# Swapping two PSUM banks in a pipelined attention stage: value transposes and value projection trade places

## The reference

```python
h = tok(x)                              # importance MLP, cumsum, pooling 750 -> 375 tokens a batch
h = h + attn(layernorm(h))              # 8 heads of 64
h = h + ffn(layernorm(h))               # 16 experts, top-k by expert, and a shared MLP
# attn, on xn = layernorm(..) * gamma + beta, padded with two zero columns in front:
y = wd0 * (W @ xn)[:-2] + wd1 * (W @ xn)[1:-1] + wd2 * (W @ xn)[2:]    # for q, k and v alike
p = softmax(q k^T * scale - slope * |i - j|, causal);  out = (p v) @ wout.T
# ffn: probs = softmax(layernorm(h) @ gate_w); each expert takes its best tokens
```

## Time and profile before

| what | value |
|---|---|
| median of 3 runs | 1337.28 us (1337.11 to 1339.53) |
| the profiled execution, its own time | 1337.11 us |
| its span, first to last instruction | 1335.4 us |
| PE busy over the span | 1181.6 us, 88% |
| PEld | 992.4 us, 74% |
| DVE | 895.8 us, 67% |
| ACT | 732.2 us, 55% |
| POOL | 405.9 us, 30% |
| mean granted TensorE clock | 0.956 of full speed |

### The profile page before, as it was taken

One profiled execution on the slowest core, in us unless ns is written; L12 is line 12 of the kernel. 1 busy time (PEld: TensorE's weight loads), 2 busy tenths in 40 slices (PEclk: granted clock), 3 DMA queues, 4 the chain that ended last, 5 costly groups with the idle time before them and its releaser, 6 DMA issues. The chain is left out here.

```text
span 1335.4 us, 23186 instructions
## 1 busy us (share of the span) xinstructions
PE 1181.6 (88%) x7812; PEld 992.4 (74%) x7812; DVE 895.8 (67%) x2614; ACT 732.2 (55%) x1845; POOL 405.9 (30%) x379
## 2 busy tenths in 40 slices
PE   6999999999978999999999999999995998766663
PEld 6999999999966777777777777777773777545552
DVE  5656566656658988888888888897874887222220
ACT  2444534344448877788877778887882432222220
POOL 5000001302011444333344323231111001688885
PEclk9999999999989999999999999999997998988876
DMA  5100000000010000000000000000002100444542
GB/s 140 31 13 24 12 24 12 18 19 12 1 36 1 19 18 17 26 26 26 25 19 11 23 27 26 25 11 11 14 16 55 30 18 19 100 91 89 90 87 23
DMA packets 91800, 42.94 MB, mean 32 GB/s; under 512 B 31066, under 2 KB 88007, under 8 KB 91687
## 3 DMA queue, kind: packets, MB, share of 16 engines
q1 hardware_dynamic: 67207, 33.49, 9.3%
q0 software_dynamic: 23808, 6.69, 3.9%
q10 hardware_dynamic: 672, 1.31, 0.3%
HBM read 28.22 MB, written 9.65 MB: 28 GB/s over the span
## 5 line engine op out<-in xcount | busy, mean ns | idle before, releaser
L487 PE MATMUL bank<-h1hl,W2hl 128*128 128x376 f32 x1536 | 277.3, 336 | 2.9 <-DVE h1hl L643 2.9
L487 PEld LDWEIGHTS bank<-h1hl,W2hl 128*128 128x128 f32 x1536 | 263.6, 189 | 7.4 <-issue 4.3
L1057 ACT ACTIVATE P<-P,nmax 125x375 f32<-125x375 f32 (+2 forms) x384 | 189.0, 501 | 1.4 <-DVE nmax L1185 1.4
L587 ACT ACTIVATE h<-bank,b2c 128x375 f32<-128x375 f32 x128 | 73.5, 575 | 207.3 <-PE bank L487 207.3
L226 POOL TENSOR_SCALAR cellmax<-grid,csb 125x375 f32<-125x375 f32 x96 | 122.7, 1288 | 206.0 <-DVE csb L219 133.1
L1185 DVE CUSTOM_DVE_ANT_0 P<-bank,nbias 125x375 f32<-125x375 f32 (+2 forms) x384 | 138.9, 410 | 2.1 <-PE bank L898 1.7
L1067 ACT COPY PT<-bank 128x500 f32<-128x500 f32 (+1 forms) x256 | 127.9, 553 | 6.5 <-PE bank L911 6.1
L898 PE MATMUL bank<-QK 64*125 64x375 f32 (+2 forms) x768 | 116.3, 407 | 4.2 <-DVE nmax L1185 3.7
L911 PE MATMUL bank<-ident,P 125*128 125x125 f32 x768 | 113.4, 275 | 0.6 <-ACT P L1057 0.4
L1075 ACT ACTIVATE tap<-bank,qkd 128x375 f32<-128x375 f32 x128 | 68.6, 571 | 79.2 <-PE bank L951 79.1
L1651 ACT ACTIVATE hE<-bank,EB 128x375 f32<-128x375 f32 x64 | 36.7, 573 | 134.8 <-PE bank L1600 132.0
(11 more groups left out here) (209 smaller groups left out, 2326.7 us busy)
## 6 DMA issues: line engine op xcount, KB each, us to landing
X<-in_x_dram SPq DMA_DIRECT2D x31, 375.0 KB
EW<-in_L_ffn_w_dram SPq DMA_DIRECT2D x32, 256.0 KB
token_table<-row SPq DMA_DIRECT2D x16, 210.9 KB
tTall<-tT SPq DMA_DIRECT2D x16, 187.5 KB, 2.5
out_dram<-oS SPq DMA_DIRECT2D x16, 187.5 KB
tTall<-in_L_tok_W_dram ACTq DMA_DIRECT2D x1, 1024.0 KB, 8.9
EB<-in_L_ffn_b_dram SPq DMA_DIRECT2D x16, 62.5 KB
tok<-token_table,ids POOLq DMA_INDIRECT x48
```

What stands on the lines that cost most here:

```text
L487: last = nc.tensor.matmul(bank[4 + m % 2][:, :NE], W2hl[:, a, k, m * 128:(m + 1) * 128], h1hl[:, p, b, k], start=(k == 0 and n == 0), stop ...
L587: nc.scalar.activation(h2[:, p, m], bank[4 + m % 2][:, :N], ACT.Gelu, bias=b2c[:, m:m + 1]).then_inc(s_g2, 1)
L1057: nc.scalar.activation(P[:, 2 * r + q, SEG[i]:SEG[i] + w], P[:, 2 * r + q, SEG[i]:SEG[i] + w], ACT.Exp, bias=nmax[:, 2 * r + q, i:i + 1], ...
```

## The change

The values trade banks, and two pieces of work move within their engines' lists:
- `transpose_v` writes G0 instead of G1 and ACT L1090 reads it there. It waits for the queries to be finished (`s_qk` 2c + 3) and no longer for the keys (2c + 4).
- `project_v` writes G1 instead of G0, waits until the keys' taps have been read out of it, and stands in PE's list behind `transpose_probs`. ACT's first tap of the values stands behind `copy_probs` accordingly, and DVE's taps read G1.
- `project_qk` swaps its waits: the queries now wait for the copied values and, for certain pairs, for the gate's reads of pTs and of the logits, and the keys wait for VT.
- The gate's transposed probabilities and logits go to G0 as well.
- `take_n2T` moves on ACT from the end of step 7 to the end of step 0 of the next body, and `split_n2T` on DVE from step 0 to step 1, ahead of `take_pooled`.

In the diff below the other edits only rename the bank: ACT's copy of the values (L1090), PE L1011 and L1039 and DVE L1268, L1283 and L1286 go from G1 to G0, and DVE's value taps (L1208, L1214) from G0 to G1.

```diff
@@ project_qk, project_v, transpose_v (PE) @@
                         if n == 0:
-                            wait(pe, s_vt, 4 * m + c)
-                        else:
                             wait(pe, s_v, 4 * m + c - 1)
                             if c == 2:
                                 wait(pe, s_pc, m - 1)
                             if c == 1:
                                 wait(pe, s_lm, 2 * (m - 1))
+                        else:
+                            wait(pe, s_vt, 4 * m + c)
...
                 def project_v(m, c, u):
-                    pe.wait_ge(s_qk, 8 * m + 2 * c + 1)
+                    pe.wait_ge(s_qk, 8 * m + 2 * c + 2)
...
-                        last = nc.tensor.matmul(G0[:, :XE], WVT[:, a, c * 128:(c + 1) * 128], xnThl[:, u, x_],
+                        last = nc.tensor.matmul(G1[:, :XE], WVT[:, a, c * 128:(c + 1) * 128], xnThl[:, u, x_],
...
                     pe.wait_ge(s_vt, 4 * m + c + 1)
-                    pe.wait_ge(s_qk, min(8 * m + 2 * c + 4, 8 * B))
+                    pe.wait_ge(s_qk, min(8 * m + 2 * c + 3, 8 * B))
...
-                        last = nc.tensor.transpose(G1[:PT_, t * 128:(t + 1) * 128], VT[:, t * PT_:(t + 1) * PT_],
+                        last = nc.tensor.transpose(G0[:PT_, t * 128:(t + 1) * 128], VT[:, t * PT_:(t + 1) * PT_],
@@ body (PE) @@
-                        if part == 1:
-                            if valid(b):
-                                transpose_v(b, c)
-                            if valid(m):
-                                project_v(m, d, m % 2)
-                        m, d = pair_before(b, c, 2)
-                        if part == 0 and valid(m):
-                            attend(m, d, u if c >= 2 else v_)
-                        m, d = pair_before(b, c, 1)
-                        if valid(m):
-                            transpose_probs(m, d, part)
+                        if part == 1 and valid(b):
+                            transpose_v(b, c)
+                        k, e = pair_before(b, c, 2)
+                        if part == 0 and valid(k):
+                            attend(k, e, u if c >= 2 else v_)
+                        k, e = pair_before(b, c, 1)
+                        if valid(k):
+                            transpose_probs(k, e, part)
+                        if part == 1 and valid(m):
+                            project_v(m, d, m % 2)
@@ body (ACT) @@
-                            if valid(m):
-                                act.wait_ge(s_vp, 4 * m + d + 1)
-                                wait(act, s_vt1, 4 * m + d)
-                                nc.scalar.activation(tap0[:, 2], G0[:, 0:N], ACT.Copy,
-                                                     scale=vd[:, d, 0:1]).then_inc(s_vt0, 1)
                         m, d = pair_before(b, c, 1)
                         if part == 1 and valid(m):
                             copy_probs(m, d, 1)
+                        k, e = next_pair(b, h)
+                        if part == 1 and valid(k):
+                            act.wait_ge(s_vp, 4 * k + e + 1)
+                            wait(act, s_vt1, 4 * k + e)
+                            nc.scalar.activation(tap0[:, 2], G1[:, 0:N], ACT.Copy,
+                                                 scale=vd[:, e, 0:1]).then_inc(s_vt0, 1)
...
-                        if h == 7 and ahead(b + 2):
-                            take_n2T(act, b + 2, G2)
+                        if h == 0 and ahead(b + 1):
+                            take_n2T(act, b + 1, G2)
@@ body (DVE) @@
-                        if h == 0 and ahead(b + 1):
+                        if h == 1 and ahead(b + 1):
                             split_n2T(dve, b + 1)

```

More of the change, by code:

```diff
@@ L1010, in body @@
                             for t in range(NT):
-                                last = nc.tensor.transpose(G1[:E, t * PT_:(t + 1) * PT_], row[:, t, C:ROW],
+                                last = nc.tensor.transpose(G0[:E, t * PT_:(t + 1) * PT_], row[:, t, C:ROW],
                                                            ident[:PT_, :PT_])
@@ L1038, in body @@
                             for t in range(NT):
-                                last = nc.tensor.matmul(G1[:PT_, t * E:(t + 1) * E], tT[:, t * PT_:(t + 1) * PT_],
+                                last = nc.tensor.matmul(G0[:PT_, t * E:(t + 1) * E], tT[:, t * PT_:(t + 1) * PT_],
                                                         gate[:], start=True, stop=True)
@@ L1090, in body @@
                                 nc.scalar.copy(V[:, b % 2, :, c * 128:(c + 1) * 128],
-                                               G1[:PT_, :NT * 128].rearrange("p (t d) -> p t d", d=128)
+                                               G0[:PT_, :NT * 128].rearrange("p (t d) -> p t d", d=128)
                                                ).then_inc(s_v, 1)
-                            if valid(m):
-                                act.wait_ge(s_vp, 4 * m + d + 1)
-                                wait(act, s_vt1, 4 * m + d)
-                                nc.scalar.activation(tap0[:, 2], G0[:, 0:N], ACT.Copy,
-                                                     scale=vd[:, d, 0:1]).then_inc(s_vt0, 1)
                         m, d = pair_before(b, c, 1)
@@ L1207, in body @@
                             dve.wait_ge(s_vt0, n + 1)
-                            nc.vector.scalar_tensor_tensor(out=tap1[:, 2], in0=G0[:, 1:N + 1], scalar=vd[:, d, 1:2],
+                            nc.vector.scalar_tensor_tensor(out=tap1[:, 2], in0=G1[:, 1:N + 1], scalar=vd[:, d, 1:2],
                                                            in1=tap0[:, 2], op0=ALU.mult, op1=ALU.add
@@ L1213, in body @@
                             wait(dve, s_vtp, n)
-                            nc.vector.scalar_tensor_tensor(out=VT[:], in0=G0[:, 2:N + 2], scalar=vd[:, d, 2:3],
+                            nc.vector.scalar_tensor_tensor(out=VT[:], in0=G1[:, 2:N + 2], scalar=vd[:, d, 2:3],
                                                            in1=tap1[:, 2], op0=ALU.mult, op1=ALU.add
@@ L1267, in body @@
                             wait(dve, s_ps, 16 * m)
-                            nc.vector.tensor_copy(pTs[:], G1[:E, :N]).then_inc(s_pc, 1)
+                            nc.vector.tensor_copy(pTs[:], G0[:E, :N]).then_inc(s_pc, 1)
                         if h == 1 and weights_ahead(b + 3):
@@ L1282, in body @@
                             dve.wait_ge(s_lp, m + 1)
-                            nc.vector.reduce_max(lmax[:], G1[:PT_, :NT * E].rearrange("p (t e) -> p t e", e=E),
+                            nc.vector.reduce_max(lmax[:], G0[:PT_, :NT * E].rearrange("p (t e) -> p t e", e=E),
                                                  AX_X).then_inc(s_lm, 1)
                             dve.wait_ge(s_lm, 2 * m + 1)
-                            nc.vector.tensor_tensor(lg[:], G1[:PT_, :NT * E].rearrange("p (t e) -> p t e", e=E),
+                            nc.vector.tensor_tensor(lg[:], G0[:PT_, :NT * E].rearrange("p (t e) -> p t e", e=E),
                                                     lmax[:, :, None].broadcast_to([PT_, NT, E]),
```

## The result

The changed kernel takes 1346.41 us (median of 5 runs, 1344.94 to 1351.32), against 1337.28 before: ratio 1.0071, 95% interval 1.0051 to 1.0090. It is slower, by more than the measurement's 0.2%. Once more on another occasion it took 1344.3 us beside 1338.9 (1.0046, 1.0030 to 1.0062). The profiled execution took 1345.23 us, 8.12 more than the one before; its span is 1343.5.

A forecast was written before the change was run, and what follows sets the result against it. The limit was taken to go round PE, DVE and ACT. Steady batches 3.5 us, batch 13 0.2 and the last two 4.3, less 1.5 at the start, made 6.5 us more: 1343.8 us, range 1333 to 1350.

The forecast's parts named there:

- four stretches: Steady batch between value transposes' starts (v1: step 1's): v5-v7, v7-v1, v1-v3, v3-v5; summed 39.63 against 39.31 us.
- The longer way to VT: From the value transposes' start to finished VT, through PE, ACT and DVE: 3.87 us instead of 3.20.
- both engines set it: Way to VT: PE's own order gives the tap at most 0.1 us less, so PE and ACT both set it.
- The queries' earlier waits: PE's query projection waits for pTs in step 2 and the logits in step 0, some 1 us each.
- The token passes: ACT, step 0: costed at nothing, with 0.5 us of cover before pooling; DVE's 1.15 us wait goes.
- PE's idle as the prize: Second stage, PE: 1.47 us of waits a batch, about 20 us over 14 batches, held not to be had.
- The start: Batches 0 and 1 have no logits to wait for in step 0 and gain 1.5 us.
- The ends: Batch 13 pays 0.2 us; the last two, without pooling to hide the longer way, 4.3 together.
- the batch before it is alike: Last but one batch: like the last one but somewhat slacker today, so 2.0 us more.
- a faster outcome: Rival: the long way to VT is hidden in steps 5 and 7; batch 38.86 us, total 1332; chance 0.18.
- No change: Rival: old waits are swapped for new ones of the same size; 0.1 us a batch, 1339; chance 0.17.
- a stall at pooling: Rival: the token passes reach pooling, 0.4 us in 13 batches, 5 us on top, 1349; chance 0.12.

The follow-up runs named there:

- the order back: Changed kernel with the value projection ahead of the probabilities' transposes on PE and the values' first tap ahead of ACT's two copies, as before the change: 1327.66 us (0.9913).
- ACT's list back: Changed kernel with only the values' first tap put back ahead of the two probability copies on ACT: 1347.08 us (1.0059).
- PE's alone: Changed kernel with only the value projection put back ahead of the probabilities' transposes on PE: 1368.33 us (1.0239).
- the swap alone: Kernel before with only the swap of G0 and G1 and the waits it brings; order and tokens as before: 1328.79 us (0.9939).
- another arrangement of the same work: Changed kernel with the old order, and keys instead of queries waiting for pTs while there is pooling: 1321.1 us (0.9865), repeated at 1320.64.
- the tokens back: Changed kernel with the normalised tokens read where they were before (ACT step 7, DVE step 0): 1345.78 us (1.0054).
- the token move: Run alone on the kernel before: tokens read by ACT at the end of step 0, split by DVE in step 1; 1324.18 us (0.9894).

## Why the prediction was right

The forecast was 6.5 us and the profiled execution shows 8.1; the median is 1346.41 where I said 1343.8, inside the range. The mechanism held. That the total came so near is partly luck: outside the steady batches the start gained 1.5 us more than forecast and the ends cost 1.4 more, and 2.2 us have no term in the sum at all.

- **The steady batch**: right in each of its four stretches: 8.18, 9.29, 12.37 and 9.79 us were forecast, 8.17, 9.32, 12.38 and 9.74 measured. Eleven batches gave 3.27 us, forecast 3.5.
- **The longer way to VT**: 3.87 forecast, 3.93 measured, and shown to be the cause by taking the order back (39.61 to 38.66 us a batch). That "both engines set it" held in its outcome, not in its detail: ACT's list back alone gave 0.1 us a batch, and PE's alone made the way longer.
- **The queries' earlier waits**: right that they come (1.2 us for the logits, 0.96 for pTs), and the pTs one costs 0.53 us, now measured. In v1 to v3 the wait for the keys' tap is outweighed by it as forecast, whether VT comes late or not (12.38 us in the change, 12.37 with the order back). What failed is my expectation for the swap alone, that the queries' wait for pTs would give back all that PE gains: the swap gains 0.47 us a batch by itself, most of it in v7 to v1.
- **The token passes** cost nothing in steady batches: right, no L252 waits for L296. That their 1.15 us would be gained was true for the kernel before (1.04), and not for the changed one, as the sum had it.
- **PE's idle as the prize**: the prediction opened with the 20 us of PE's waits and held that they were not to be had. This change didn't get them, but another arrangement of the same work came 18 us under the kernel before (1320.64 against 1338.9), so PE's own work was not what forbade it.
- **The start**: batches 0 and 1 were to gain 1.5 us. From the first projection to v1 of batch 2 the gain is 3.0, about 1.5 of it the clock. Against this stand the 2.2 us ahead of the stage, for which the sum has no term. In all it is 3.27 - 3.00 + 5.92 + 2.20 - 0.29 = 8.10 (batches 2 to 12, the start, batches 13 to 15, ahead of the stage, behind it), where the forecast had 3.5 - 1.5 + 4.5 = 6.5.
- **The ends**: undersized. Batches 13 to 15 were put at 4.5 us (0.2 + 4.3) and took 5.9 (0.45 + 4.13 + 1.34). Batch 15's two links were 8.80 and 8.87, forecast 8.86 and 8.92. The term that failed is "the batch before it is alike": its v1 to v3 is 11.03 us, and not 8.9. PE and DVE there:

```profile
942.79 0.90 PE L898 MATMUL bank<-QK 64*125 64x375 f32 x4
945.67 1.90 PE L951 MATMUL bank<-xnThl,WQKT 128*128 128x378 f32 x6 [1.98 <-DVE pTs L1268]
947.50 2.44 PE L931 MATMUL bank<-PT,V 125*64 125x375 f32 x12
```
```profile
944.53 0.54 DVE L302 TENSOR_TENSOR xnThl<-xnT,xnThl 128x375 fp32r<-128x375 f32 x1
944.99 0.53 DVE L1268 COPY pTs<-bank 16x375 f32<-16x375 f32 x1
```

The split (L302) stands between VT and pTs and the token passes ahead of the value copy, and PE waits 1.98 us. Then the projections take 1.90 us instead of 1.3 and attend 2.44 instead of 1.49. The windows say why:

```profile
943.00:945.00 2.00, 0.69 (x4) 0.09 (x2) 1.60 (x4) 2.00 (x9) 0.00 (x0) 1.00 0.13 39
...
948.00:950.00 2.00, 2.00 (x13) 0.98 (x10) 1.66 (x4) 1.35 (x5) 0.00 (x0) 0.63 0.00 0
```

The clock was 1.00 up to 945 us, and 0.63 in the stretch behind the idle one. In the run with the tokens back the same place has a wait of 1.19 us and no slower matmuls, as its timeline of PE shows:

```profile
947.26 1.28 PE L951 MATMUL bank<-xnThl,WQKT 128*128 128x378 f32 x6 [1.19 <-DVE pTs L1268]
948.46 1.49 PE L931 MATMUL bank<-PT,V 125*64 125x375 f32 x12
```

The difference to that run's 8.88 us is 2.15. From v1 to the projection it is 5.10 us here and 4.52 there, so 0.6 are the passes and the split; from the projection to v3 it is 5.93 and 4.36, so about 1.6 are the clock. The repeat of the changed kernel has 11.06 us at the same place.
- **The rivals**: a faster outcome needed a way to VT under 3.5 us; with the order back it is 3.50 us, and the batch 38.66 (forecast for it 38.86). No change and a stall at pooling are excluded by the 0.30 us and by the missing wait.

## What to carry to other kernels

Moving a producer behind other work to spare its engine a wait moves everything that hangs on it: add up the way from its first input to the buffer that the next round waits for, across all engines, before counting the idle time that goes. In a loop that goes round three engines, parts don't add: the token move was worth some 14 us alone, about 3 with the bank swap (the second stage of the two profiles; the medians are 1 us apart) and nothing with bank swap and order together, so try each part of a bundle by itself. Two that were gains were lost here by the third.

## What the runs showed of the hardware that I had not expected

A new PE wait of about 1.2 us, repeated each batch, usually costs only itself, but sometimes the clock falls behind it. In the run with ACT's list back, v7 to v1 was 9.25 us in most batches and 10.8 in four of batches 1 to 12. One of these, PE and the windows around it:

```profile
501.40 1.96 PE L951 MATMUL bank<-xnThl,WQKT 128*128 128x378 f32 x6 [1.16 <-DVE lg L1285]
503.29 2.38 PE L931 MATMUL bank<-PT,V 125*64 125x375 f32 x12
```
```profile
495.00:501.00 6.00, 5.25 (x42) 4.10 (x40) 5.79 (x18) 5.64 (x17) 0.00 (x0) 1.00 0.16 46
501.00:504.00 3.00, 2.60 (x10) 1.82 (x12) 2.53 (x10) 2.48 (x9) 0.00 (x0) 0.62 0.35 105
504.00:506.00 2.00, 2.00 (x16) 1.19 (x13) 1.90 (x7) 1.15 (x4) 0.00 (x0) 0.71 0.02 5
506.00:510.00 4.00, 4.00 (x36) 3.68 (x35) 1.72 (x11) 3.50 (x8) 0.00 (x0) 1.00 0.19 54
```

The granted clock is 1.00, then 0.62 and 0.71, then 1.00 again: matmuls of 2.4 and of 1.2 GHz mixed, for some 1.55 us of loss. Batches with the same wait of 1.2 us and no fall stand beside it. In batches 1 to 12 the repeat of the changed kernel had two falls (10.89 and 10.87 us instead of 9.32) and its first profile none; behind the wait of 2 us in batch 14 both had one. The same shows in the first stage: PE waits 0.6 us there at about 182 us in both profiles compared, and the clock fell in the changed kernel's alone, down to 0.50 from 186 to 188 us. The changed kernel's executions spread over 6 us and those before over 3; the two slowest, 1351.32 and 1348.24 us, have a mean clock of 0.948 and 0.950, the other three 0.955 and 0.956. That fits falls of the clock, but these two were not profiled. The Trainium skill ("TensorE: Matmul & The Clock Gate", Part 1) says that a gate passes half of the pulses when PE has not been busy enough of late; the two levels agree with the rows here.
